# Transposes of B moved behind the first matmul of a projection, and one semaphore increment per block of small matmuls

## What is computed

```python
proj = u @ W_in.T                       # u: (4, 512, 256) after layer norm and modulation
xBC, z, A_log = jnp.split(proj, [CONV_DIM, CONV_DIM + D_INNER], axis=-1)
xBC = depthwise_causal_conv(xBC, conv_w, 4 taps) + conv_b
x, Bm, Cm = jnp.split(xBC, ...)         # x: 32 heads x 8, Bm and Cm: 32 heads x 64
a = -softplus(A_log)
Lm = exp(segsum(a))                     # lower triangle of decays
M = einsum('blhn,bshn,bhls->bhls', Cm, Bm, Lm)
y = einsum('bhls,bshp->blhp', M, x) + D * x
out = y * silu(z + z_bias) @ W_out.T
```

## Time and profile before

| | before |
|---|---|
| median of 3 runs | 585.75 us (585.65 to 586.25) |
| profiled execution, its own time | 584.53 us |
| its span | 582.7 us |
| TensorE busy | 563.0 us, 97% |
| VectorE busy | 472.7 us, 81% |
| ScalarE busy | 386.8 us, 66% |
| GpSimd busy | 206.2 us, 35% |
| granted TensorE clock, mean | 0.994 of full |

### The profile page before, as it was taken

The page is one execution under the profiler, slowest core; times in us unless marked ns, Lnnn a source line. Parts: engine busy times, 40 slices in busy tenths (PEclk is TensorE's granted clock), DMA queues, the critical chain, the costliest instruction groups (busy, mean ns, idle before and its releaser), DMA issues.

```text
span 582.7 us, 18096 instructions
## 1 busy us (share of the span) xinstructions
PE 563.0 (97%) x6693; PEld 452.1 (78%) x6694; DVE 472.7 (81%) x753; ACT 386.8 (66%) x960; POOL 206.2 (35%) x377
## 2 busy tenths in 40 slices
PE   7899999999999999999999999999998998998997
PEld 3577677778778787777777877877687987988987
DVE  6789999989989989988999999999657637637443
ACT  2588788788888888877878888887633223332340
POOL 4742265464464365686245243445000000000000
PEclk9799999999999999999999999999999999999999
DMA  8535544533534535533443447456423034100101
GB/s 288 231 115 191 152 142 121 163 116 114 163 106 126 162 108 194 165 109 108 132 147 112 126 151 192 149 162 176 133 74 108 1 97 120 37 2 0 37 0 37
DMA packets 39516, 70.93 MB, mean 122 GB/s; under 512 B 4532, under 2 KB 10804, under 8 KB 39224
## 3 DMA queue, kind: packets, MB, share of 16 engines
q1 hardware_dynamic: 39480, 70.47, 38.6%
HBM read 57.34 MB, written 13.12 MB: 121 GB/s over the span
## 4 chain that ended last, share of the span: by engine, by line
PE 81%; DVE 9%; ACT 3%; issue 3%; DMA 2%; POOL 1%; SPq 0%; DVEq 0%; ACTq 0%; POOLq 0%
PE ps L334 17%; PE ps L336 16%; PE ps L335 16%; PE ps L499 10%; PE ps L543 5%; PE ps L482 4%; PE ps L534 4%; PE ps L518 4%; PE ps L603 2%; DVE acc L1054 2%; DMA u_sb<-in_u 1%; DVE mix L1042 1%; DVE hid_lo L1190 1%; PE ps L356 1%; PE ps L387 1%
## 5 line engine op out<-in xcount | busy, mean ns | idle before, releaser
L1054 DVE SCALAR_TENSOR_TENSOR acc<-ps,cw_dve,acc 128x511 f32<-128x511 f32 (+2 forms) x384 | 259.1, 739 | 2.9 <-ACT acc L751 1.4
L789 ACT ACTIVATE decay<-sums,p_slot 128x128 f32<-128x128 f32 x512 | 160.6, 396 | 1.3 <-DVE mix L1042 0.5
L1317 POOL TENSOR_SCALAR_AFFINE_SELECT sums<-sums 128x512 f32<-128x512 f32 x128 | 81.6, 640 | 180.6 <-DMA sums<-running_sums 172.7
L751 ACT ACTIVATE acc<-ps,cw_act 128x512 f32<-128x512 f32 x128 | 93.2, 776 | 48.9 <-PE ps L543 45.4
L334 PE MATMUL ps<-ht_hi,wg_hi 128*128 128x512 f32 x256 | 106.9, 418 | 2.0 <-POOL wg_lo L1255 1.1
L336 PE MATMUL ps<-ht_hi,wg_lo 128*128 128x512 f32 x256 | 101.1, 395 | 0.0
L335 PE MATMUL ps<-ht_lo,wg_hi 128*128 128x512 f32 x256 | 101.0, 395 | 0.0
L1042 DVE TENSOR_TENSOR mix<-ps,decay 128x1024 f32<-128x1024 f32 x64 | 78.0, 1219 | 20.6 <-PE ps L499 19.3
L499 PE MATMUL ps<-acc 64*64 64x64 f32 (+1 forms) x2048 | 69.8, 255 | 0.7 <-DVE mix L1042 0.7
L889 ACT ACTIVATE silu_sb<-ps 128x512 f32<-128x512 f32 x32 | 19.2, 599 | 77.3 <-PE ps L336 77.3
L499 PEld LDWEIGHTS ps<-acc 64*64 64x64 f32 x2048 | 54.4, 132 | 9.7 <-issue 9.0
(11 more groups left out here) (136 smaller groups left out, 897.4 us busy)
## 6 DMA issues: line engine op xcount, KB each, us to landing
sums<-running_sums SPq DMA_DIRECT2D x128, 256.0 KB, 3.3
y_parts<-yt_sb SPq DMA_DIRECT2D x32, 256.0 KB, 2.0
wg_raw<-in_w_bc SPq DMA_DIRECT2D x8, 512.0 KB, 4.6
stage<-y_parts SPq DMA_DIRECT2D x16, 256.0 KB, 4.2
u_sb<-in_u SPq DMA_DIRECT2D x4, 512.0 KB, 7.1
stage<-in_w SPq DMA_DIRECT2D x1, 2048.0 KB, 15.3
x_channels<-acc SPq DMA_DIRECT2D x8, 256.0 KB, 2.3
ee<-decay_rows SPq DMA_DIRECT2D x8, 256.0 KB, 4.4
```

What stands on the lines that cost most here:

```text
L751: af(acc[:, b % 2, t, :], ps[:, PROJ_BANK[t], :], ACT.Identity, bias=cw_act[:, t, 1:2], scale=cw_act[:, t, 0:1]).then_inc(s[f"tap_a{t}"], 1)
L789: i = af(decay[:, j, c * P:(c + 1) * P], sums[:, j, c * P:(c + 1) * P], ACT.Exp, scale=-1.0, bias=p_slot[:, b * CH + c, j:j + 1])
L1054: stt(a[:, d:], ps[:, PROJ_BANK[t], 0:L - d], cw_dve[:, t, TAPS - 1 - d:TAPS - d], a[:, d:], ALU.mult, ALU.add).then_inc(s[f"taps{t}"], 1)
L1317: gp.affine_select(out=v, in_=v, compare_op=ALU.is_ge, fill=FAR, base=0, pattern=[[0, CH], [1, P]], channel_multiplier=-1).then_inc(s["mas ...
```

## The change

Three things are done; the matmuls, copies, activations and transfers themselves stay the same.

1. `proj` is cut in two: `proj_first`, the first of the six matmuls, and `proj_rest`, the other five. The transposes of tile 0 stand between the first and the second matmul of the projection of tile 0. The transposes of tile 1 of unit q leave the end of the step and stand in the next step (where the unit is r) between the first and the second matmul of the projection of tile 1, in front of `states(r)`. In the tail they stand ahead of the z projection.
2. `scores`, `states` and `intra` increment their semaphore once, on the last matmul, and all waits for them count accordingly. So that the last matmul is a 128-column one, `scores` runs its two column halves in the other order.
3. On ScalarE `decays(q, 3)` and the copy of `b_tok` tile 1 change places.

```diff
@@ -424,7 +424,8 @@
-            def proj(g, b, t):
+            def proj_first(g, b, t):
                 n = g * B + b
@@ -432,11 +433,19 @@
                     pe.wait_ge(s["w_split"], (g * GT + PLACE[t]) * 2 + 2)
-                for kt in range(KT):
-                    i = split_mm(ps[:, PROJ_BANK[t], :], wg_hi[:, t, kt, :], wg_lo[:, t, kt, :],
-                                 ht_hi[:, kt, b * L:(b + 1) * L], ht_lo[:, kt, b * L:(b + 1) * L],
-                                 kt == 0, kt == KT - 1)
-                i.then_inc(s[f"proj{t}"], 1)
+                mm(ps[:, PROJ_BANK[t], :], wg_hi[:, t, 0, :], ht_hi[:, 0, b * L:(b + 1) * L], start=True, stop=False)
+            def proj_rest(g, b, t):
+                o = ps[:, PROJ_BANK[t], :]
+                mm(o, wg_hi[:, t, 0, :], ht_lo[:, 0, b * L:(b + 1) * L], start=False, stop=False)
+                mm(o, wg_lo[:, t, 0, :], ht_hi[:, 0, b * L:(b + 1) * L], start=False, stop=False)
+                split_mm(o, wg_hi[:, t, 1, :], wg_lo[:, t, 1, :], ht_hi[:, 1, b * L:(b + 1) * L],
+                         ht_lo[:, 1, b * L:(b + 1) * L], False, True).then_inc(s[f"proj{t}"], 1)
+            def proj(g, b, t):
+                proj_first(g, b, t)
+                proj_rest(g, b, t)
@@ -493,15 +502,14 @@
                 for c in range(CH):
-                    for h in range(2):
+                    for h in (1, 0):
                         for a in range(2):
...
                                    start=True, stop=True)
-                            if c == CH - 1:
-                                i.then_inc(s["score"], 1)
+                i.then_inc(s["score"], 1)
@@ -518,8 +526,7 @@
                                    start=(c == 0), stop=(c == CH - 2), skip_group_check=True)
-                            if p and c == CH - 2:
-                                i.then_inc(s["state"], 1)
+                i.then_inc(s["state"], 1)
@@ -542,8 +549,7 @@
                                mix[:, j, c * P:(c + 1) * P], start=False, stop=True, skip_group_check=True)
-                        if c == CH - 1:
-                            i.then_inc(s["intra"], 1)
+                i.then_inc(s["intra"], 1)
@@ -574,19 +580,22 @@
                 first = r is None
-                proj(g, b, 1)
+                proj_first(g, b, 1)
+                if r is not None:
+                    b_transposes(r, br, 1, False)
+                proj_rest(g, b, 1)
                 if r is not None:
...
                     scores(r, br, 1, False)
+                proj_first(g, b, 0)
                 b_transposes(q, bq, 0, first)
-                proj(g, b, 0)
+                proj_rest(g, b, 0)
                 proj(g, b, 3)
...
                 scores(q, bq, 0, first)
-                b_transposes(q, bq, 1, first)
@@ -653,6 +662,7 @@
             pe.wait_ge(s["wz_split"], 2)
+            b_transposes(q, B - 2, 1, False)
             z_project(0, 0)
@@ -744,9 +754,9 @@
                     if t == 1:
-                        act.wait_ge(s["score"], 8 * (n - 1))
+                        act.wait_ge(s["score"], 2 * (n - 1))
                     elif t:
-                        act.wait_ge(s["intra"], JH * (n - 1))
+                        act.wait_ge(s["intra"], n - 1)
                 act.wait_ge(s[f"proj{t}"], n + 1)
@@ -791,14 +801,14 @@
             def state_copies(r):
-                act.wait_ge(s["state"], 2 * r + 2)
+                act.wait_ge(s["state"], r + 1)
                 for a in range(2):
...
             def y_evacuate(r, half, before):
-                act.wait_ge(s["intra"], JH * r + JH)
+                act.wait_ge(s["intra"], r + 1)
                 if not (isinstance(before, int) and before == 0):
@@ -843,8 +853,8 @@
                     y_evacuate(r, b % 2, gr * 2 + (b - 2) % B // 2)
+                decays(q, bq, 3, first)
                 b_evacuate(q, 1)
-                decays(q, bq, 3, first)
@@ -1035,10 +1045,10 @@
-                dve.wait_ge(s["score"], 8 * q + 4 * p + 4)
+                dve.wait_ge(s["score"], 2 * q + p + 1)
                 dve.wait_ge(s["exp_done"], 4 * q + 2 * p + 2)
                 if not first:
-                    dve.wait_ge(s["intra"], JH * q)
+                    dve.wait_ge(s["intra"], q)
                 tt(mix[:, 2 * p:2 * p + 2, :], ps[:, 2:4, :], decay[:, 2 * p:2 * p + 2, :],
@@ -1294,7 +1304,7 @@
                 if not early:
-                    await_unit("state", 2 * (n - 1))
+                    await_unit("state", n - 1)
                 for c in range(CH - 1):
...
```

More of the change, by code:

```diff
@@ L872, in h2_parts @@
                     if b == 0:
-                        act.wait_ge(s["intra"], JH * NG * B)
+                        act.wait_ge(s["intra"], NG * B)
                     af(h32b[:, kt, :], ps[:, (6 if b else 0) + kt, :], ACT.Identity, bias=shift[:, 1, kt, b:b + 1],
@@ L1308, in own_x @@
                 if not early:
-                    await_unit("intra", JH * (n - 1))
+                    await_unit("intra", n - 1)
                 x = x_tok[:, b * CH:(b + 1) * CH, bass.ds(g * GC, GC)]
```

## The result

| | before | after |
|---|---|---|
| median | 585.7 us (585.1 to 586.25, 4 runs) | 610.29 us (609.13 to 611.79, 4 runs) |
| ratio to before | | 1.0422, 95% interval 1.0396 to 1.0447 |
| profiled execution, its own time | 584.53 us | 609.98 us |
| its span | 582.7 us | 608.0 us |

The changed kernel is 4.2% slower, 24.6 us by the medians. Forecast were 611.1 us and a range from 604.5 to 617.

What follows compares the result with a forecast made beforehand. TensorE was taken to bound the kernel. Stalls 23.8, transposes 1.6, column order 0.3, GpSimd wait -0.5, and first and last steps 0.1 sum to 25.3 us more: 611.1 us, range 604.5 to 617.

Steps and rivals of the forecast that it cites:

- The stall: TensorE in front of `states`, waiting for ScalarE's `b_tok` copy: 0.85 us in each of 28 steps, 23.8 us.
- the direct cost: Outside the stall: moved transposes of tile 0, 1.6 us, and the new order of `scores` column halves, 0.3 us.
- the chain: End of `intra` to `states`: first tap 0.04, taps and y copy 1.80, decays 1.17, copy 0.50, release 0.17; sum 3.68 us.
- The tap behind `intra`: ScalarE's first tap would start 0.04 us after `intra` ends, in place of 0.15.
- The release of TensorE: From the end of the `b_tok` copy to `states`: taken as 0.17 us, with 0.15 and 0.26 as bounds.
- The increments: Four to one on `intra`: the waiting ScalarE gets 0.11 us back, some 0.035 per further increment; no cost on TensorE.
- The transposes' move: Behind the first projection matmul: exposes 0.11 us where 0.06 was, 0.05 lost, 1.6 us over 31 times for tile 0.
- the row of the tail: A projection matmul straight behind `intra`'s small tiles in the tail takes 0.34 us in place of 0.23.
- The GpSimd wait: TensorE's wait near 262 us for GpSimd's split of new weights would vanish: 0.5 us less, or 0 if not.
- The copy in time: Rival: the `b_tok` copy ends early enough, no stall, moved transposes save 9 us, total 576.6 us; chance 0.03.
- The larger stall: Rival: increments give nothing back and the release costs 0.26; stall 1.05 us a step, total 616.7 us; chance 0.10.
- The smaller stall: Rival: earlier release or transposes saving part of 0.09; stall 0.7 us, no direct loss, total 604.8 us; chance 0.10.

Runs made afterwards that it cites:

- the kernel with the copy first: Changed kernel with ScalarE's order undone, the copy of `b_tok` tile 1 ahead of `decays(q, 3)` again: 589.11 us, ratio 1.0055.
- half: Changed kernel with the copy of `b_tok` tile 1 between the second and third of the four `decays(q, 3)` activations: 595.39 us, ratio 1.0168.
- moved ahead: Changed kernel with `decays(q, 3)` ahead of the taps of tiles 3 and 2, in ScalarE's idle time before `intra`: 589.37 us, ratio 1.0055.
- the first version: Kernel before with GpSimd's whole third butterfly of the second feed-forward weight moved one step later: 585.61 us, ratio 1.0001.
- the third: Kernel before with GpSimd's whole third butterfly one group later, behind that group's second step: 584.87 us, ratio 0.9982.

## Why the prediction was right

**The stall: the step that carried it, right in mechanism and size.** Forecast were 0.85 a step (3.68 - 2.83), 23.8 in all. In the changed kernel `states` starts 3.67 behind `intra`, which is 0.84 later than before. Without a stall it would start at 2.89, as the kernel with the copy first shows. So of the 0.84 are 0.78 a stall and 0.06 the direct cost of the moved transposes and of the new order, which the forecast had inside the stall too; a whole step has 0.11 of direct cost. By the chip the two lines on ScalarE alone are worth 24.6 - 3.6 = 21.0 us on top of the other edits (some 22.8 of stalls, less the 1.58 of the wait for GpSimd that they hide), and 26.2 on the kernel before, where the increments are longer and no direct cost lies inside the stall. Three ways of taking the decays out from between `intra` and the copy (undone, half, moved ahead) gave what the chain of the rows said.

**Parts of the chain that were off, and cancelled.** The tap behind `intra` was put at 0.04 and is at 0.07: the price of an increment, read from different instructions, did not carry over in full. The release of TensorE was put at 0.17 and is at 0.14; the decays take 1.18 and the copy 0.48, where 1.17 and 0.50 were taken. The sum was right to 0.01 by that luck.

**The increments: direction right, term too large.** 0.11 forecast, 0.07 to 0.08 measured. By the rows they take back some 2 us in the changed kernel, and nothing in the kernel before.

**The transposes' move: a loss as forecast, a little too large.** 0.05 each time forecast, 0.04 measured; 1.6 for tile 0, and 1.05 measured on the chip. From the start of `scores` to the third projection matmul are 218.62 - 216.69 = 1.93 in the changed kernel, and 206.77 - 204.89 = 1.88 before, of which 0.01 is the new order. The three transposes take 218.31 - 218.06 = 0.25 in place of 206.22 - 205.91 = 0.31, and the projection matmul now in front takes 0.34 where one behind another takes 0.24: 0.06 gained, 0.10 lost. The 0.34 (218.06 - 217.72) are what the row of the tail had promised.

**The GpSimd wait:** gone in the changed kernel, as forecast. The step there takes 11.97 like the others, where it took 12.42.

**A term that was not in the sum.** In the profiled execution of the changed kernel the first `states` starts at 63.64, before at 62.44. Of these 1.2, 1.0 lie ahead of the first projection matmul, in instructions that the change doesn't touch. In the profiles of the ten other kernels that stage ends between 42.3 and 44.7 us. It is the variation of single executions, and no effect of the change. Then come 0.7 up to the next `states` (13.28 in place of 12.62, the first stall), 23.8 for the 28 steps behind it (334.9 from 76.9 to 411.8, before 311.1), and -0.4 for the tail and the feed-forward part. For those 29 steps the forecast has some 25.0 (stall, direct cost and the GpSimd wait), and 24.5 are measured; that the 23.8 here is the figure forecast for the stalls alone is a coincidence. So the span's 25.3 us, just the forecast sum, are partly chance; the medians' difference of 24.6 is the better measure of it.

**The rivals.** The copy in time (576.6) is refuted by the runs: it needs the decays elsewhere, and even then the move costs 3.6 and saves nothing. The larger stall (616.7) fell with the release, which was at its lower bound, and with the increments, which do give something back. The smaller stall (604.8) wanted 0.7 a step and no direct loss, or part of the drain saved; measured are 0.78 and a direct loss, and moving the transposes of tile 0 alone made the kernel before slower.

## What to carry to other kernels

An engine with 34% of idle time can still bind: ask what stands between the event that it waits for and the result that others wait for, and how much later than that result its user starts. Here this cover was 0.38 us less the release of 0.14, and 1.17 us of work that nobody waits for just then, put in each step ahead of a copy that TensorE waits for, cost 21 us in all; the same work in the idle time ahead of the event cost nothing. Before work is moved between two groups of matmuls, compare what the first instruction behind a change of array tiles exposes: by the rows a transpose cost 0.06 extra there and a 512-column projection matmul 0.10 to 0.11, and the run with tile 0 alone confirms the difference of 0.04.

## What the runs showed of the hardware

I had not expected a VectorE copy of 128x12 elements to take 2.2 us in place of 0.17. It did so both times when a 2.4 us GpSimd operation on SBUF had started 0.2 us earlier, it ended within 0.03 us of that operation, and it took 0.17 again when the operation was moved away. The kernel before shows it at a smaller scale, where the same copy took 0.45 and ended at 269.16, 0.02 behind a GpSimd operation of 0.64 (268.50 + 0.64 = 269.14):

```profile
268.71 0.45 DVE L1088 COPY cw_dve<-conv_sb 128x12 f32 x1 [0.17 <-DVE acc L1054]
...
268.50 0.64 POOL L1317 TENSOR_SCALAR_AFFINE_SELECT sums<-sums 128x512 f32<-128x512 f32 x1
```

A short instruction of VectorE can so wait until a long one of GpSimd has ended. The Trainium skill, "SBUF — State Buffer", section "SBUF: two separate sides", says that VectorE and GpSimd share a pair of ports which whoever starts first holds for the whole instruction, and that on VectorE this concerns instructions in a two-port mode (it names fp32 copies within SBUF) or with two SBUF inputs. The traces agree with it for this copy. Not every VectorE instruction was held: six taps of the convolution in a row (L1054), which read PSUM and SBUF, took 4.03 in the first version, with GpSimd's second operation of 2.37 beside them, and 4.03 in the third, with no GpSimd operation longer than 0.64 beside them.

A single increment of `intra` reached ScalarE 0.07 behind its modelled end, that of a projection 0.04. Why the two differ stays open.
